# Recurrent layer with windowed attention and routed experts: in which late steps GpSimd adds the score mask

## The reference, cut to what matters

```python
xn = layernorm(x)
q, k, v = split(xn @ qkv_w.T)
attn = (q @ k.T) * hd ** -0.5
attn = where(m != 0, attn * m, -inf)
s = (softmax(attn) @ v) @ proj_w.T + proj_b
e = argmax(xn @ router_w)
xs = xn * sigmoid(max(xn @ router_w))
routed = (silu(xs @ gate_w[e]) * (xs @ up_w[e])) @ down_w[e]
shared = (silu(xn @ shared_gate_w) * (xn @ shared_up_w)) @ shared_down_w
out = x + s * silu(routed + shared)
```

## Time and profile before

| what | value |
|---|---|
| median of 3 runs | 599.69 us (599.25 to 600.19) |
| the profiled execution's own time | 600.95 us |
| its span | 599.1 us |
| busy share PE, PEld, DVE, ACT, POOL | 91%, 79%, 73%, 40%, 43% |
| chain that ended last, by engine | PE 60%, DVE 13%, POOL 8%, issue 6%, DMA 5%, ACT 4% |
| mask add L426 | 28 instructions, mean 1677 ns; DVE's maximum waited for it 21 times, 11.7 us |
| subtraction L432 | 64 instructions, median 1448 ns, up to 2617 ns |
| scaling L708 | 64 instructions, median 941 ns, the last one starts at 574.38 us |
| indirect DMA L442 | 32 issues, 3.9 us in the median from issue to landing |
| mean granted clock of TensorE | 0.976 of full speed |

### The profile page before, as it was taken

How to read it: one execution, slowest core, us unless ns; L and a number is a source line. 1 busy time by engine, 2 the same in 40 slices (tenths; PEclk the granted TensorE clock), 3 DMA queues, 4 the chain that set the end, 5 groups by cost and what they waited for, 6 DMA issues and landing times.

```text
span 599.1 us, 10330 instructions
## 1 busy us (share of the span) xinstructions
PE 546.0 (91%) x3302; PEld 474.1 (79%) x3302; DVE 439.2 (73%) x1029; ACT 240.3 (40%) x506; POOL 255.5 (43%) x188
## 2 busy tenths in 40 slices
PE   1989999979988999999999999999999999898952
PEld 1757789858867899989899988899879788786941
DVE  6777858898768557566566466646899999999862
ACT  1464454536652443442433433342535434352210
POOL 7133324038885223223323322320476795974630
PEclk9989999989998999999999999999999999999977
DMA  9624534235625666766566756563235664754421
GB/s 302 208 80 156 187 106 124 88 96 176 186 95 166 202 188 200 217 189 197 174 189 199 219 175 204 156 171 102 44 63 74 92 89 60 104 76 64 70 44 19
DMA packets 106345, 83.17 MB, mean 139 GB/s; under 512 B 42164, under 2 KB 104500, under 8 KB 106164
## 3 DMA queue, kind: packets, MB, share of 16 engines
q1 hardware_dynamic: 90180, 64.81, 36.9%
q0 software_dynamic: 10496, 12.59, 12.7%
q10 hardware_dynamic: 5616, 5.11, 2.5%
HBM read 59.41 MB, written 27.26 MB: 145 GB/s over the span
## 4 chain that ended last, share of the span: by engine, by line
PE 60%; DVE 13%; POOL 8%; issue 6%; DMA 5%; ACT 4%; SPq 1%; ACTq 0%; POOLq 0%; DVEq 0%
PE psV L939 11%; PE psM L989 11%; PE psS L914 8%; PE psM L998 5%; PE psM L966 5%; PE psM L925 4%; PE psM L961 4%; PE psM L889 4%; DMA xnT<-ys_dram,slot 4%; PE psM L894 3%; POOL xnT L442 3%; POOL Sx L432 3%; PE psM L947 2%; DVE O L760 2%; DVE Sx L708 2%
## 5 line engine op out<-in xcount | busy, mean ns | idle before, releaser
L432 POOL TENSOR_TENSOR Sx<-Sx,mx 128x752 f32<-128x752 f32 x64 | 100.6, 1571 | 122.5 <-DVE mx L718 122.1
L939 PE MATMUL psV<-VB,PTs 128*128 128x132 f32 x1024 | 134.8, 285 | 17.8 <-DVE O L760 17.6
L939 PEld LDWEIGHTS psV<-VB,PTs 128*128 128x128 f32 x1024 | 129.2, 195 | 22.4 <-issue 21.0
L426 POOL TENSOR_TENSOR Sx<-Sx,cst 128x752 f32<-128x752 f32 x28 | 47.0, 1677 | 183.4 <-DVE Sx L708 183.4
L914 PE MATMUL psS<-kBD,qBD 128*128 128x188 f32 x512 | 97.8, 323 | 0.2 <-DVE Sx L708 0.2
L914 PEld LDWEIGHTS psS<-kBD,qBD 128*128 128x128 f32 x512 | 84.7, 190 | 9.6 <-issue 2.5
L740 DVE STREAM_TRANSPOSE PTs<-Sx 128x512 f32<-128x512 f32 x128 | 82.8, 685 | 4.2 <-ACT Sx L497 4.2
L708 DVE TENSOR_TENSOR Sx<-psS,cst 128x752 f32<-128x752 f32 x64 | 60.0, 938 | 30.6 <-PE psS L914 30.2
L989 PE MATMUL psM<-xT,EB 128*128 128x128 f32 x624 | 76.5, 276 | 0.6 <-DMA EB<-in_L_ffn_up_w 0.6
L760 DVE TENSOR_TENSOR O<-psV,rs 32x128 f32<-32x128 f32 x256 | 73.5, 287 | 4.8
L989 PEld LDWEIGHTS psM<-xT,EB 128*128 128x128 f32 x624 | 73.8, 192 | 3.0 <-ACT qBD L486 1.3
(11 more groups left out here) (106 smaller groups left out, 688.6 us busy)
## 6 DMA issues: line engine op xcount, KB each, us to landing
EB<-in_L_ffn_gate_w SPq DMA_DIRECT2D x39, 256.0 KB, 3.1
EB<-in_L_ffn_up_w SPq DMA_DIRECT2D x39, 256.0 KB, 3.6
EB<-in_L_ffn_down_w SPq DMA_DIRECT2D x39, 256.0 KB, 3.0
VB<-v_dram SPq DMA_DIRECT2D x256, 32.0 KB
stage<-xs_dram SPq DMA_DIRECT2D x39, 128.0 KB, 2.2
ys_dram<-yb ACTq DMA_DIRECT2D x39, 128.0 KB, 3.1
xs_dram<-blank SPq DMA_DIRECT2D x9, 512.0 KB, 3.2
v_dram<-vS SPq DMA_DIRECT2D x8, 512.0 KB, 3.0
```

Of the source, the lines that this page charges most:

```text
L432: nc.gpsimd.tensor_tensor(s, s, mx[n % 3][:, :].unsqueeze(2).broadcast_to([P, 2 * G, KW]), ALU.subtract).then_inc(a_sub, 1)
L939: last = mm(psV[:, j, at:at + HS * VW], PTs[n % 2][:, k, j, i, :], VB[n % 2][:, i, k, :, VW * j:VW * j + VW], start=k == 0, stop=k == 1)
```

## The change

`masked_late` becomes true for further steps: those from 38 on after which no chunk's silu stands, which are the steps in which GpSimd issues no gather.

```diff
 def masked_late(n):
-    return n < BATCH or E0 <= n < E0 + NP
+    return n < BATCH or E0 <= n < E0 + NP or n >= E0 + NP and not silu_at(n + 1)
```

## The result

The changed kernel takes 607.16 us in the median of five runs (606.33 to 607.75); the kernel before took 599.57 us beside it. The ratio is 1.0124, with a 95% interval of 1.0108 to 1.0140: slower by 7.6 us, where 7.4 were forecast (607.1).

The account below looks back on a forecast made before the run. TensorE was taken to bound to about 467 us, VectorE from there on; delays of 0, 1.38, 0.53, 1.18, 1.83, 0.53, 1.43 and 0.53 sum to 7.4 us on 599.69, giving 607.1 us, range 602.2 to 611.0.

Parts of the forecast that it names:

- the 0.6 us of the forecast: Steps 38 to 43, TensorE bound: fewer mask matmuls bring VectorE 0.6 us forward by step 43.
- 0.53 us where GpSimd is free: Late step with GpSimd free: reciprocal 3.57 us behind the scaling instead of 3.04, all of it VectorE waiting.
- 0.04 + 1.66 + 0.03 + 0.86 us: Late step behind GpSimd's DMA issues: start delay, mask add, maximum's start, reciprocal; 2.59 us after the last issue.
- 38 to 46: Steps 38 to 46: VectorE's lead, step 43's +0.53 and the gather at step 46 leave delay 0.
- The delay reaches the end whole: Step 47 to the end: gathers, transfers, tanh and value matmuls shift along, so all 7.4 us reach the end.
- step 43's 0.53 us: Step 43, GpSimd free: VectorE delayed by 0.53 us, net about 0 against the 0.6 us lead.
- that gather was issued behind a GpSimd chain that hasn't moved: Step 46: silu needs ScalarE's tanh of 467.41, which waits for a gather; any lead left is cancelled, delay 0.
- Step 47: Gather's second issue ends at 471.57, so the reciprocal comes at 474.16 against 472.78: +1.38 us.
- Step 62: Issue ends at 569.55, reciprocal at 572.14 against 569.07: +3.07 us, less 1.64 of a later wait, +1.43.
- the 1.64 us of its later slack: Step 62: VectorE waited 1.64 us at 572.59 for a gather's tanh, which absorbs that much of the delay.
- step 55: Issue ends at 523.09, so the reciprocal comes at 525.68 against 524.50: +1.18 us.
- Clock: Wider TensorE gaps at steps 47/48, 55/56, 58/59 drop it to 1.2 GHz: 609.8 us, two falls 612.5; chance 0.10.

Follow-up runs that it names:

- both_engines: Changed kernel, but TensorE keeps its 20 mask matmuls in the new late steps and GpSimd adds a tile of zeros there; 607.52 us, ratio 1.0135.
- matmuls_out: Kernel before without the 20 mask matmuls in the ten steps and without any mask add in their place; 599.65 us, ratio 1.0001.
- the two groups of steps: Kernel before with the mask moved only in 38, 39, 43, 51, 59, 63 (600.98 us), or only in 47, 55, 58, 62 (605.09 us).
- out_behind: Changed kernel, but GpSimd issues step 57's output DMA behind step 58's subtraction; 605.21 us, ratio 1.0098.
- the second profile: Kernel before, unchanged, profiled once more, without the clock fall; median 599.58 us, ratio 1.0006, profiled execution 599.08 us.
- the first profile: Kernel before, unchanged, the profile the forecast was made against, with a clock fall at 552 us; profiled execution 600.95 us.
- queued_steps: Kernel before with the mask moved only in steps 47, 55, 58 and 62, behind GpSimd's DMA issues; 605.09 us, ratio 1.0089.

## Why the prediction was right

It went by three claims, and the runs bear out each.

*VectorE binds from 467 us on, and TensorE's saving is worth nothing there.* Shown by both_engines and matmuls_out; ahead of 467 us it is worth the 0.6 us of the forecast.

*A late step costs 0.53 us where GpSimd is free, and 0.04 + 1.66 + 0.03 + 0.86 us behind the last issue where it isn't.* Shown by the two groups of steps, by out_behind, and by the rows above. Against the second profile, and from step 37 on, the steps cost:

| step | forecast | measured | wait ahead of the maximum |
|---|---|---|---|
| 38 to 46 | 0 | 0.01 | 0.56 in step 43 |
| 47 | 1.38 | 1.09 | 1.34 |
| 51 | 0.53 | 0.54 | 0.55 |
| 55 | 1.18 | 1.07 | 1.08 |
| 58 | 1.83 | 1.84 | 2.41 |
| 59 | 0.53 | 0.56 | 0.56 |
| 62 | 1.43 | 1.27 | 3.10 |
| 63 | 0.53 | 0.55 | 0.56 |
| sum | 7.4 | 6.9 | |

(The measured column is the difference of neighbouring columns of the table above, 47 to 48 and so on, in the first row 37 to 47, in the last from step 63's scaling to the issue of the last output DMA. That issue in the changed kernel and in the second profile:

```profile
597.52 1.21 POOL L419 DMA_DIRECT2D out<-X  x1 [11.06 <-DVE X L800]
...
589.35 1.21 POOL L419 DMA_DIRECT2D out<-X  x1 [12.25 <-DVE X L800]
```

It comes 8.17 us later. Less the 1.16 of step 37 that is 7.0 us, the sum with the small shares between the steps. The two spans differ by 7.9 only, since the rest of the execution behind that issue is 0.3 us shorter.)

*The delay reaches the end whole.* Shown by the table of scalings, which never falls back by more than 0.2 us after step 47.

The step that looked weakest held too. For step 43's 0.53 us the forecast had a lead of 0.6 to set against it, and for the rest of the lead "that gather was issued behind a GpSimd chain that hasn't moved". Against the second profile, and less the 1.16 of step 37, VectorE is 0.62 us early at step 42, 0.08 at step 44 and 0.82 at step 46, where it no longer waits for TensorE's scores. GpSimd's gather issue at 461.84, which stands 1.09 us behind, and ScalarE's tanh at 467.80, 1.20 behind, have not moved by more than 0.07. So the silu of step 46 has to wait, and the lead is gone:

```profile
468.46 0.69 DVE L793 SCALAR_TENSOR_TENSOR xnT<-EB,xnT 128x512 f32<-128x512 f32 x1 [0.68 <-ACT EB L542]
```

The parts that were mis-sized are smaller. Step 47 came out 0.3 us cheaper than forecast: its reciprocal was 1.30 us later relative to its scaling, and VectorE made up 0.2 of that in the rest of the step. Step 62 came out 0.16 cheaper because more than the 1.64 us of its later slack was used up, step 55 0.11. These take the sum from 7.4 to 6.9, and nothing cancels them. The last scaling was forecast near 581.3 us and starts at 580.07, and the span is 605.2 for 606.5.

So the forecast of 7.4 us is 0.4 above what this pair of profiles shows and 0.2 below what the medians show (7.6 us, with 6.5 to 8.4 as its interval). That it lies so near the medians is in part luck, since executions of the same program differ by more than that.

It also rests on a choice: the sum was taken from the median of the runs and not only from the profiled execution. From that one it was 608.4, and the changed kernel's profile shows 607.14, because the first profile had a clock fall that the changed one hasn't.

The rival *Clock* didn't come about in the profiled execution of the changed kernel at the places where it was forecast, though the gaps did grow. TensorE's groups of value matmuls behind them, in the changed kernel:

```profile
550.38 2.08 PE L939 MATMUL psV<-VB,PTs 128*128 128x132 f32 x16 [2.55 <-DVE O L760]
558.02 2.08 PE L939 MATMUL psV<-VB,PTs 128*128 128x132 f32 x16 [2.26 <-DVE O L760]
...
578.13 3.86 PE L939 MATMUL psV<-VB,PTs 128*128 128x132 f32 x16 [4.52 <-DVE O L760]
585.27 3.86 PE L939 MATMUL psV<-VB,PTs 128*128 128x132 f32 x16 [3.28 <-DVE O L760]
```

2.08 us behind gaps of 2.55 and 2.26, both longer than the 1.89 that had preceded the 2.89 in the earlier trace rows. Only behind 4.52 us did the clock fall, a group earlier than before, and that group was not what VectorE waited for. In the profile of both_engines, whose gaps are like these, the group at 550.23 took 3.56 us behind a gap of 2.24, and the next scaling came no later for it. So even where the fall came about it added nothing to that delay. The Trainium skill ("TensorE: Matmul & The Clock Gate", section "HAM oscillation — how this bites in real kernels") says that idle gaps bring the array back to its lower clock. The traces agree in part: a fall followed the gap of 4.52 us here and the one of 1.89 in the earlier trace rows, and none followed those of 2.55 and 2.26.

## What to carry to other kernels

Before work is moved to an engine that "has time", look at what stands ahead of it in that engine's queue at the moment when its input is ready: of the 7.4 us of the forecast, 4.8 stood for DMA issues ahead of the mask add and only 2.7 for its own length, and of the 6.9 that the profiles show, some 4.2 are the queue's share by the same reckoning. Work taken from an engine that waits anyway is worth next to nothing (of 3.2 us of matmuls here about 0.6, in the steps in which TensorE was still the bound), and a new wait on the engine that binds counts in full unless that engine has a wait of its own later in the same step. And of two operations of which the second reads what the first wrote, the pair came out a little cheaper here with another between them, as long as nobody waited for the second.

When two profiles are compared, look first at how far apart they are ahead of the first step that was changed. Here it was 1.16 us, and read as an effect it would have put a cost of 0.63 us on steps that cost nothing.

## What the runs showed of the hardware that was not expected

- Having two VectorE operations that depend on each other side by side cost 0.15 us a step here: 3.04 us for scaling, maximum and transpose, 2.89 for scaling, transpose and maximum.
- The same program in two executions: a gap of TensorE of 1.9 us led to half clock once (2.89 us for 16 matmuls) and not the other time (2.08), and gaps of 2.55 and 2.26 us didn't in the changed kernel. Two variants had a gap of 2.24 us there; one ran 3.56 us behind it (both_engines), the other 2.08 (queued_steps). One such fall made an execution some 1.2 us longer, about a sixth of what was to be explained. A single profile can be off by that much.
- The rows of GpSimd's mask adds can begin 1.1 us inside the row of a DMA issue (step 58), but they end as if they had begun at its end: 1.70 us after it in step 47, 1.69 in step 58.
